# Flamingo attention on one core: probabilities times values as three fp32r products, heads turned ahead of the projection

## What is computed

```python
def _gqa(q, k, v):
    scale = 1.0 / np.sqrt(q.shape[-1])
    scores = jnp.einsum('bsghd,btgd->bghst', q, k) * scale
    p = jax.nn.softmax(scores, axis=-1)
    return jnp.einsum('bghst,btgd->bsghd', p, v)

core = _gqa(q, k, v).reshape(b, s, nh * d)          # self attention
xout = _gqa(qx, kx, vx).reshape(b, s, nh * d)       # attention to the context
cat = jnp.concatenate([core, xout], axis=-1)
catq = _div_clamp_fp8(cat, proj_smooth)             # rounded to fp8 steps
return jnp.einsum('bsi,oi->bso', catq, wproj) * (proj_in_scale * proj_w_scale)
```

## Time and profile before

| | us |
|---|---|
| median of 3 runs | 1647.15 (1645.8 to 1648.83) |
| profiled execution, its own time | 1652.13 |
| its span | 1650.4 |
| TensorE busy | 1600.4 (97%) |
| VectorE busy | 1086.7 (66%) |
| ScalarE busy | 1011.8 (61%) |
| GpSimd busy | 485.7 (29%) |
| granted TensorE clock, mean | 0.994 of full speed |

### The profile page before, as it was taken

One profiled execution on the slowest core, in us unless ns is written; L12 is line 12 of the kernel. 1 busy time (PEld: TensorE's weight loads), 2 busy tenths in 40 slices (PEclk: granted clock), 3 DMA queues, 4 the chain that ended last, 5 costly groups with the idle time before them and its releaser, 6 DMA issues.

```text
span 1650.4 us, 26832 instructions
## 1 busy us (share of the span) xinstructions
PE 1600.4 (97%) x9136; PEld 1220.9 (74%) x9136; DVE 1086.7 (66%) x2124; ACT 1011.8 (61%) x2855; POOL 485.7 (29%) x515
## 2 busy tenths in 40 slices
PE   7989979999999999999999999999999999999998
PEld 6878766666767777777677777777777777777887
DVE  6358855444986677777787776666666666788322
ACT  3354335553467887777777877767767777775100
POOL 1000222223524334334243343343433433420000
PEclk9999989999999999999999999999999999999999
DMA  8030648885673242363243262121142121110011
GB/s 300 26 109 27 242 170 264 278 260 159 219 223 110 84 147 72 105 246 112 75 141 109 87 213 97 45 76 57 45 183 79 46 108 44 55 42 1 26 39 39
DMA packets 75810, 196.59 MB, mean 119 GB/s; under 512 B 6896, under 2 KB 27376, under 8 KB 69168
## 3 DMA queue, kind: packets, MB, share of 16 engines
q1 hardware_dynamic: 70016, 176.50, 31.1%
q0 software_dynamic: 5680, 18.62, 3.9%
HBM read 147.12 MB, written 47.97 MB: 118 GB/s over the span
## 4 chain that ended last, share of the span: by engine, by line
PE 75%; DVE 6%; ACT 4%; DMA 1%; issue 1%; POOL 1%; another core or an unknown queue 0%; DVEq 0%; POOLq 0%; SPq 0%; ACTq 0%
PE bank L2514 9%; PE bank L2515 9%; PE bank L2576 7%; PE bank L99 6%; PE bank L101 6%; PE bank L100 6%; PE bank L2594 6%; PE bank L2607 6%; PE bank L2565 5%; PE bank L1423 4%; PE bank L1443 4%; PE bank L2586 3%; DVE x_res L1782 1%; PE bank L1403 1%; ACT t_sc L2720 1%
## 5 line engine op out<-in xcount | busy, mean ns | idle before, releaser
L2514 PE MATMUL bank<-t_half,t_xh 128*128 128x256 f16 (+1 forms) x1024 | 309.3, 326 | 0.7 <-DVE t_hn L2825 0.7
L2515 PE MATMUL bank<-t_half,t_xh 128*128 128x256 f16 (+1 forms) x1024 | 306.0, 326 | 0.0
L2825 DVE TENSOR_TENSOR t_hn<-bank,t_rs 128x256 f32<-128x256 f32 (+1 forms) x256 | 130.8, 553 | 159.4 <-POOL t_rs L2479 69.5
L2476 POOL TENSOR_SCALAR t_ve<-t_ss 128x4 f32<-128x4 f32 (+1 forms) x128 | 25.9, 202 | 597.8 <-DVE t_ss L2821 589.9
L2720 ACT ACTIVATE t_sc<-bank,t_mx 128x128 f32<-128x128 f32 x512 | 183.8, 455 | 4.7 <-DVE t_mx L2845 4.7
L2479 POOL TENSOR_TENSOR t_rs<-t_ve,t_mhalf 128x4 f32<-128x4 f32 (+1 forms) x128 | 171.0, 1336 | 10.6
L2720 ACT ACTIVATION_READ_ACCUMULATOR t_sc<-bank,t_mx 128x1 f32 x512 | 151.8, 297 | 0.0
L2514 PEld LDWEIGHTS bank<-t_half,t_xh 128*128 128x128 f16 x1024 | 100.3, 98 | 66.7 <-issue 1.4
L2515 PEld LDWEIGHTS bank<-t_half,t_xh 128*128 128x128 f16 x1024 | 100.2, 98 | 66.0
L2758 ACT ACTIVATE t_y<-bank,smooth 128x128 bf16<-128x128 f32 x512 | 139.2, 400 | 1.9 <-PE bank L2594 1.9
L2576 PE MATMUL bank<-t_hT 128*128 128x128 f32 x1024 | 131.0, 281 | 2.3 <-ACT t_hT L2747 2.3
(11 more groups left out here) (348 smaller groups left out, 3544.9 us busy)
## 6 DMA issues: line engine op xcount, KB each, us to landing
t_xh<-xq_scratch SPq DMA_DIRECT2D x64, 512.0 KB, 3.3
t_cr<-in_ctxT_dram SPq DMA_DIRECT2D x64, 256.0 KB, 2.7
t_half<-w_half SPq DMA_DIRECT2D x12, 1024.0 KB, 7.7
y_rows<-s_y SPq DMA_DIRECT2D x39, 256.0 KB
e_w<-in_w_units_dram SPq DMA_DIRECT2D x8, 1024.0 KB, 12.0
w_rows<-in_w_qkv_dram SPq DMA_DIRECT2D x8, 1024.0 KB, 6.4
xq_scratch<-z_xs SPq DMA_DIRECT2D x16, 512.0 KB, 3.9
t_slot<-w_plain SPq DMA_DIRECT2D x4, 2048.0 KB, 8.2
```

What stands on the lines that cost most here:

```text
L2514: nc.tensor.matmul(out, rows[:, k, kind, :], w[0][:, k, a:b], start=k == 0, stop=False)
L2515: last = nc.tensor.matmul(out, rows[:, k, kind, :], w[1][:, k, a:b], start=False, stop=k == KT - 1)
```

## The change

Probabilities and values are each kept as a high fp32r part and a low fp32r part, and their product is three fp32r products instead of one fp32 product. The low parts are made by VectorE (`values_low`, `probs_low`), from the PSUM banks that hold the full numbers. `attend` waits for the low part of the probabilities (`ptl_in`). On TensorE `turn` of i now comes ahead of `output` of i-3. In the last steps `probs_low` is put ahead of roundings. The buffer `xn` of the dense stage is laid out anew, since the low parts of the values lie where one of its halves was.

```diff
+        even = at("xn0", 151, [P, J, D])
+        self.xn = [even, at("xn1", wqx + 8, [P, J, D]), even, at("xn3", 160, [P, J, D])]
-        self.xn = [at(f"xn{i}", kb, [P, J, D]) for i, kb in enumerate((151, 160))]
...
-    pT = sb("pT", 108, [P, KH, P])
-    vv = [sb(f"vv{i}", 112 + 2 * i, [P, 2 * QG, P]) for i in range(2)]
+    pT = sb("pT", 108, [P, KH, P], F32R)
+    pT_lo = sb("pT_lo", 100, [P, KH, P], F32R)
+    vv = [sb(f"vv{i}", 112 + 2 * i, [P, 2 * QG, P], F32R) for i in range(2)]
+    vv_lo = [sb(f"vv_lo{i}", 160 + 2 * i, [P, 2 * QG, P], F32R) for i in range(2)]
...
         def attend(m, par):
             for part in range(2):
-                pe.wait_ge(pt_in, m * 2 + part + 1)
+                pe.wait_ge(ptl_in, m * 2 + part + 1)
                 for g in range(QG):
-                    h = (1 - part) * QH + 2 * g
-                    last = nc.tensor.matmul(bank[6 + part][:, g * 256:(g + 1) * 256],
-                                            vv[par][:, (1 - part) * QG + g, :], pT[:, h:h + 2, :],
-                                            start=True, stop=True)
+                    h, v = (1 - part) * QH + 2 * g, (1 - part) * QG + g
+                    last = three_products(nc, bank[6 + part][:, g * 256:(g + 1) * 256], vv[par][:, v, :],
+                                          vv_lo[par][:, v, :], pT[:, h:h + 2, :], pT_lo[:, h:h + 2, :], True, True)
                 last.then_inc(pv_ps, 1)
...
+            if has(i):
+                turn(i)
             if has(i - 3):
                 output(i - 3, 1 - par, min(i, M) * 2 if isinstance(i, int) else i * 2, quarter)
-            if has(i):
-                turn(i)
             if has(i - 1):
                 attend(i - 1, 1 - par)
...
+        def values_low(m, par):
+            dve.wait_ge(vcp_in, m * 2 + 2)
+            if later(m, 2):
+                dve.wait_ge(pv_ps, m * 2 - 2)
+            nc.vector.scalar_tensor_tensor(vv_lo[par][:, 0:QG, :], b3[2][:, 2:4, :], env.sigma[:, 3:4],
+                                           vv[par][:, 0:QG, :].bitcast(FP32), ALU.mult, ALU.subtract)
+            nc.vector.tensor_tensor(vv_lo[par][:, QG:2 * QG, :], b3[3][:, 2:4, :],
+                                    vv[par][:, QG:2 * QG, :].bitcast(FP32), ALU.subtract)
+
+        def probs_low(m):
+            for part in range(2):
+                dve.wait_ge(pt_in, m * 2 + part + 1)
+                if part == 0 and later(m, 1):
+                    dve.wait_ge(pv_ps, m * 2)
+                nc.vector.tensor_tensor(pT_lo[:, side(part), :], b3[6 + part][:], pT[:, side(part), :].bitcast(FP32),
+                                        ALU.subtract).then_inc(ptl_in, 1)
+
         def normalise_a(m):
             dve.wait_ge(rs_in, m * 2 + 1)
-            dve.wait_ge(vcp_in, m * 2 + 2)
...
             if has(i):
                 normalise_b(i)
+            if has(i - 1):
+                probs_low(i - 1)
             if has(i + 1):
                 sums_a(i + 1)
...
             if has(i + 1):
+                values_low(i + 1, 1 - par)
                 normalise_a(i + 1)
...
             de.x_lo(dve, 0, range(2))
-            rounded(M - 3, 1 - M % 2, 0)
+            probs_low(M - 2)
             normalise_b(M - 1)
             de.x_lo(dve, 0, range(2, KT))
+            rounded(M - 3, 1 - M % 2, 0)
             rounded(M - 3, 1 - M % 2, 1)
...
             rounded(M - 2, M % 2, 0)
+            probs_low(M - 1)
             de.h_low(dve, 0, 1)
```

More of the change, by code:

```diff
@@ L2005, in normalise @@
             t = c * J + j
-            self.nc.vector.tensor_scalar(self.xn[c % 2][:, j, :], env.x_res[:, t, :], env.mv[:, t, 0:1],
+            self.nc.vector.tensor_scalar(self.xn[c][:, j, :], env.x_res[:, t, :], env.mv[:, t, 0:1],
                                          env.rstd[:, t:t + 1], ALU.subtract, ALU.mult).then_inc(self.normed, 1)
@@ L2016, in turn @@
             for j in range(J):
-                last = self.nc.tensor.transpose(self.bank[2 + k % 2][:, ramp(j)], self.xn[c % 2][:, j, ramp(k)],
+                last = self.nc.tensor.transpose(self.bank[2 + k % 2][:, ramp(j)], self.xn[c][:, j, ramp(k)],
                                                 self.env.ident[:])
@@ L2310, in attention @@
     (cr_in, xh_in0, xh_in1, chi_in, clo_in, a_ps, b_ps, sqa_in, vcp_in, sqb_in,
-     red, ve_in, rs_in, n_in, t_ps, e_in, s_ps, mx_in, ex_in, sum_in, pn_in, pt_ps, pt_in, pv_ps, y_in,
+     red, ve_in, rs_in, n_in, t_ps, e_in, s_ps, mx_in, ex_in, sum_in, pn_in, pt_ps, pt_in, ptl_in, pv_ps, y_in,
      rnd, cq_in, pj_ps, x_in, half_in, wp_in, wraw_in, kv_w, kvx_w, q_w, qx_w) = (
@@ L2315, in attention @@
              "b_ps", "sqa_in", "vcp_in", "sqb_in", "red", "ve_in", "rs_in", "n_in", "t_ps", "e_in", "s_ps",
-             "mx_in", "ex_in", "sum_in", "pn_in", "pt_ps", "pt_in", "pv_ps", "y_in", "rnd", "cq_in",
+             "mx_in", "ex_in", "sum_in", "pn_in", "pt_ps", "pt_in", "ptl_in", "pv_ps", "y_in", "rnd", "cq_in",
              "pj_ps", "x_in", "half_in", "wp_in", "wraw_in", "kv_w", "kvx_w", "q_w", "qx_w")])))
@@ L2950, in vector @@
         sums_a(0)
+        values_low(0, 0)
         normalise_a(0)
```

## The result

The changed kernel takes 1670.5 us (median of 4 runs, 1667.83 to 1673.07); the kernel before took 1646.47 us beside it (1645.32 to 1648.83). The ratio is 1.0142, 95% interval 1.0129 to 1.0154. The profiled execution took 1669.49 us, its span is 1667.8.

A forecast was written before the change was run, and what follows sets the result against it. TensorE bound the 15.52 us step; the new order would make a 15.72 us ring the bound. Terms 11 + 4 + 1.4 + 2 + 1 + 1 made about 20 us: 1667 us, 8-in-10 range 1650 to 1684.

The forecast's parts named there:

- a ring through ScalarE's copy of the values: Plain attention step: chain through ScalarE, VectorE, GpSimd and back to TensorE, forecast at 15.72 us against 15.52 before.
- Plain steps: Attention steps without extra work: 0.20 us longer each, 11 us for 56 of them.
- E: Moment in a step when TensorE starts the scores, the next work after probabilities times values; times are counted from it.
- the two last terms: Stretch from the query normalisation's start through turned heads and projection to the products' end: 1.40 + 0.44 + 1.72 and 1.44 us.
- late weights: Steps with centred late weights in front of the normalisation: 8 x 0.1 = 1 us more.
- Products: Probabilities times values on TensorE: 12 fp32r matmuls at 0.12 us, 1.44 us a sample, 0.30 less than before.
- Low part of the probabilities: `probs_low` on VectorE after the query normalisation: some 1.28 us, hidden by the projection.
- The clamp: VectorE's first clamp (L1299), 1.25 us before: starts behind GpSimd's low part of the context, back at 0.3 us.
- Low part of the values: `values_low` on VectorE ahead of the key normalisation: 0.75 us of work, exponentials 0.37 us later.
- Openings of a quarter: Three steps behind quarter openings, with ScalarE's projection-weight copy: 1.4 us more each, 4 in all, plus 2 for a clock fall.
- Early steps: First quarter's steps: 1.4 us more, for the one step behind ScalarE's copy of the projection weights.
- The case for faster: Rival: loop through the values less tight, TensorE stays the bound; 18 us saved, 6 given back, about 1635; chance 0.14.

The follow-up runs named there:

- The order alone: Kernel before the change, with only `turn(i)` put ahead of `output(i - 3)`, fp32 products and no low parts: 1668.6 us, ratio 1.0128.
- the projection cut in two: Changed kernel with four of the projection's matmuls ahead of the turned heads and four behind them: 1638.6 us, ratio 0.9934.
- The kernel with the projection first: Changed kernel with the projection of i-3 put back ahead of the turned heads of i: 1650.6 us, ratio 1.0022.
- the low part behind the maxima: Changed kernel with the values' low part moved on VectorE behind the maxima of the next step: 1651.7 us, ratio 1.0021.
- only early steps were edited: Changed kernel with the rounding of the previous stage's last rows moved behind the maxima in early steps: 1666.5 us, ratio 1.0093.

## Why the prediction was right, point by point

**Direction and cause.** Right. The forecast said that the earlier turned heads close a ring through ScalarE's copy of the values. The order alone makes a loss of 1.28% where the whole change makes 1.42%, and taking either the order or the values' low part off the ring recovers about 20 us.

**Plain steps.** 15.72 us forecast, 15.60 measured, 15.63 to 15.70 in hardware loops. The ring without `values_low` was said not to fit by 0.13 us; the order alone showed 0.14. Of the terms, the exponentials came at E+3.15 (3.19 forecast), the query normalisation 7.46 us later (7.53), and the two last terms together were 4.99 (5.00). The sum for these steps, 11 us (and 1 more for late weights), was 7.1 measured, of which 0.9 in the last one.

**Products.** 0.12 us each was right: ten intervals from 1030.02 to 1031.21 make 0.119. The first one behind the f16 projection takes 0.30, but starts 0.18 early, so that projection and products together are 3.15 us (3.16 forecast). The Trainium skill (TensorE: Matmul & The Clock Gate, Back-to-back issue gap) would give 0.109 as an estimate for such a product; the trace has 9% more, and the measurement decides. One row under this term was read wrongly: "0.118 per record in the scores" held a wait. The 16 records of the scores took 1.89 us there and take 1.78 in the changed kernel (1031.33 to 1033.11), 0.111 each.

**Low part of the probabilities.** Right that it is hidden: leaving it out gained nothing. The clamp behind it is back at 0.28 us (1029.34), as said: it no longer runs beside GpSimd's low part of the context, which now ends at 1029.25.

**Low part of the values.** Forecast at 0.37 us on the ring; 0.32 measured at the exponentials (3.15 against 2.83) and 0.23 in the step.

**Openings of a quarter.** Over-sized: 1.4 us each and 2 for one more fall of the clock, 2.7 us measured for the three. The two steps at full clock came to 18.2, not 18.7 us. The fall had the wrong price and the wrong count. Its 1.9 us came from 19.19 - 17.30, two different openings, and the first one can be longer by itself: with the projection cut in two it takes 18.10 us at full clock, the others 17.36.

```profile
790.27:808.37 18.10, 15.49 (x102) 11.58 (x100) 16.51 (x35) 11.93 (x38) 6.87 (x8) 1.00 0.27 81
```

The same step with and without a fall differs by 1.3 to 1.7 us, and there were three more falls, not one, all of them in the first seven steps.

**Early steps.** The term that failed. I gave them 1.4 us, for the step behind ScalarE's copy of the projection weights, and they cost 11.2. That step alone cost 3.0 (16.89 to 19.93), with a fall of the clock that wasn't counted there. Nearly all of the rest, 8.1, lies in three later steps whose ring holds the rounding of the stage before. The step of my working that was missing: I took the DVE sequence of one plain step as that of all, and did not look at what `step` puts between the key normalisation and the maxima in the first steps. Before the change those 2.06 us cost little: 0.38 of them were hidden under ScalarE's scaling, and the rest fell into the 1.6 us of slack. On a closed ring they count in full (17.68 us for the step at full clock, 15.61 + 2.07), and in the two longest of these steps the clock fell as well. Moving them took 7.4 us off again. That the total came out near is luck: plain steps and openings were put too high by about as much.

**The case for faster.** Its price was wrong. "They close the step without a hole" was my reading of the earlier trace rows; there was a hole of 0.13 us at the scores (0.11 of it inside their 1.89 us) that starts of matmuls don't show as a gap. TensorE's own sum is 15.09 us, not 15.22, and in the old order the products' gain is lost at the scores entirely (15.50). So that rival's 18 us could not have come from a shorter ring alone.

The moved `xn` buffers were not tried by themselves. The kernel with the projection first has them and is 0.2% from the kernel before, and the one with the order alone lacks them and is 1.3% slower, so they make no large part of the loss.

## What to carry to other kernels

Before moving work on the busiest engine, write down each ring that goes once round the step through the other engines, with its slack at the point that moves; a move gives slack to one ring and takes it from another, and cutting the moved piece in two can serve both. An engine whose pieces close up without idle time may still wait: look at the weight loads' waits and compare a piece's length with the same piece elsewhere. Do this for the unusual steps too (first steps, openings, loops), since their extra work counts in full once a ring has no slack.

## What the runs showed of the hardware

- Steps inside hardware loops were longer than the same steps written out only where the values' low part lay on the closed ring: 15.63 to 15.70 us against 15.60, with 0.16 to 0.22 us of idle time at the turned heads. In the two loop steps looked at, the exponentials start 3.18 and 3.24 us behind E where it is 3.15 in a written-out step. With the order alone (15.60 to 15.69 in and out of loops) and with the low part behind the maxima (15.37) the ring binds too, and steps in loops take what the others take, as they did before the change (15.51). What in the loop costs the time was not tried.
- The clock's fall to the level of 1.2 GHz behind a long stall is not fixed for a given stall: the second opening went without one in the changed kernel (18.21 us) and with one when only early steps were edited (19.56). Where the same step is on record with and without, the fall cost 1.3 to 1.7 us.
- The first fp32r product behind f16 matmuls is followed after 0.30 us, the others after 0.119. No time is lost by it: its start stands 0.18 us early in the trace.
